# Gate scores of the tokens on VectorE instead of TensorE, in a cross-attention and mixture-of-experts kernel on one core

## What is computed

```python
x = x + xattn(layernorm(x), ctx_768, w_q, w_k, w_v, w_o, b_o)   # 64 x 128 tokens of 256; 16 heads of 64
x = x + ffn(layernorm(x), gate, W1, b1, W2, b2)

def xattn(x, context, ...):
    q, k, v = x @ w_q, context @ w_k, context @ w_v
    attn = softmax(q k^T * SCALE)
    return (attn v) @ w_o + b_o

def ffn(x, gate, ...):
    raw_gate = softmax(x @ gate)                 # 8 experts
    keep the two best, divide by their sum
    return sum over the two experts of weight * (relu(x @ W1[e] + b1[e]) @ W2[e] + b2[e])
```

## Time and profile before

| what | value |
|---|---|
| time, median of 3 runs | 1654.01 us (1653.54 to 1655.09) |
| the profiled execution: its time, its span | 1657.4 us, 1655.6 us |
| mean granted TensorE clock | 0.995 |
| busy PE, DVE, ACT, POOL | 1619.5, 1267.8, 1188.3, 808.9 us |
| TensorE in the chain that ended last | 70% of the span |
| the eight gate products, L1459 | 256 products, passes -1 to 30, first at 22.7 us, last at 1150.6 us |

### The profile page before, as it was taken

How to read it: one execution, slowest core, us unless ns; L and a number is a source line. 1 busy time by engine, 2 the same in 40 slices (tenths; PEclk the granted TensorE clock), 3 DMA queues, 4 the chain that set the end, 5 groups by cost and what they waited for, 6 DMA issues and landing times.

```text
span 1655.6 us, 44861 instructions
## 1 busy us (share of the span) xinstructions
PE 1619.5 (98%) x13844; PEld 1540.7 (93%) x13845; DVE 1267.8 (77%) x3309; ACT 1188.3 (72%) x3485; POOL 808.9 (49%) x920
## 2 busy tenths in 40 slices
PE   6999999999999999999999999999799999999997
PEld 6899999999999999999999999999799999999997
DVE  6677888777788877777887777778678777777775
ACT  5777777777777777777777777777566777777674
POOL 4244454454444445444444544444436555555555
PEclk9999999999999999999999999999999999999999
DMA  8032111112211111221111122111489855555554
GB/s 266 16 90 71 57 57 57 57 65 93 71 57 57 57 57 64 87 78 58 57 57 57 64 80 83 61 57 45 148 240 260 180 88 89 82 89 88 84 85 63
DMA packets 106299, 144.01 MB, mean 87 GB/s; under 512 B 12752, under 2 KB 88656, under 8 KB 106128
## 3 DMA queue, kind: packets, MB, share of 16 engines
q1 hardware_dynamic: 60800, 87.95, 16.4%
q0 software_dynamic: 26816, 37.32, 12.8%
q10 hardware_dynamic: 18640, 18.19, 4.1%
HBM read 76.05 MB, written 67.38 MB: 87 GB/s over the span
## 4 chain that ended last, share of the span: by engine, by line
PE 70%; issue 7%; DVE 7%; DMA 5%; DVEq 3%; POOL 2%; ACT 2%; POOLq 1%; ACTq 1%; SPq 0%
PE bank_a L1362 33%; PE bank_s L1362 11%; PE bank_t L1369 8%; PE bank_v L1395 8%; DMA out<-stage_room,number 5%; DVE hid L1290 3%; DVE stage_room L1307 3%; PE bank_a L1427 2%; PE bank_a L1428 2%; PE bank_a L1435 2%; PE bank_a L1436 2%; PE bank_a L1459 2%; DVEq L1302 1%; POOL out L713 1%; DVEq L1281 1%
## 5 line engine op out<-in xcount | busy, mean ns | idle before, releaser
L642 POOL TENSOR_TENSOR prob<-prob,inv 128x512 f32<-128x512 f32 x256 | 271.1, 1059 | 600.6 <-DVE inv L937 597.5
L755 ACT ACTIVATE prob<-bank_s,low 128x128 f32<-128x128 f32 x1024 | 361.7, 367 | 189.5 <-DVE low L932 186.1
L932 DVE TENSOR_REDUCE low<-bank_s 128x4 f32<-128x512 f32 x256 | 176.3, 689 | 208.9 <-PE bank_s L1362 206.4
L713 POOL DMA_INDIRECT out<-stage_room,number x142 | 230.8, 1625 | 53.8 <-issue 53.2
L755 ACT ACTIVATION_READ_ACCUMULATOR prob<-bank_s,low 128x1 f32 x1024 | 210.7, 206 | 0.0
L866 ACT ACTIVATE hidt_h<-hid 128x512 fp32r<-128x512 f32 x142 | 89.7, 632 | 125.7 <-DVE hid L1290 123.8
L959 DVE TENSOR_TENSOR kt_l<-bank_a,kt_h 64x512 fp32r<-64x512 f32 x256 | 173.3, 677 | 3.1 <-ACT kt_h L772 1.2
L1369 PE MATMUL bank_t<-ident,prob 128*128 128x128 f32 x1024 | 161.0, 280 | 9.6 <-POOL prob L642 9.5
L1362 PE MATMUL bank_s<-kt_l,qt_h 128*128 128x256 f32 x512 | 165.3, 323 | 0.0
L748 ACT ACTIVATE probt<-bank_t 128x512 f32<-128x512 f32 x256 | 152.8, 597 | 8.6 <-issue 6.2
L772 ACT ACTIVATE kt_h<-bank_a 64x512 fp32r<-64x512 f32 x256 | 151.5, 592 | 4.9 <-PE bank_a L1362 3.4
(11 more groups left out here) (227 smaller groups left out, 5291.8 us busy)
## 6 DMA issues: line engine op xcount, KB each, us to landing
stage_room<-lists ACTq DMA_DIRECT2D x67, 265.0 KB
halves<-stage_room SPq DMA_DIRECT2D x32, 512.0 KB
homes<-halves SPq DMA_DIRECT2D x16, 1024.0 KB, 5.6
xin<-in_x SPq DMA_DIRECT2D x32, 256.0 KB, 2.7
stage_room<-in_x SPq DMA_DIRECT2D x32, 256.0 KB
stage_room<-in_w SPq DMA_DIRECT2D x32, 256.0 KB, 4.1
out<-stage_room SPq DMA_DIRECT2D x32, 256.0 KB, 2.2
cin<-in_ctx SPq DMA_DIRECT2D x32, 128.0 KB, 2.4
```

The lines of the kernel that those rows point to most:

```text
L642: pool.tensor_tensor(prob[:, n % 4, :, :], prob[:, n % 4, :, :], wide(inv[:, n % 4, :], P), ALU.mult).then_inc(s_norm.sem, 1)
L713: pool.indirect_dma_start(out, bass.IndirectOffsetOnAxis(ap=number[:, u, b:b + 1], axis=0), ysum[:, u, b, :], None, compute_op=ALU.add).th ...
L755: e = act.activation(prob[:, n % 4, h, :], bank_s[n % 2][:, h * P:(h + 1) * P], ACT.Exp, bias=low[:, n % 4, h:h + 1], scale=-1.0, accum_ou ...
L932: dve.tensor_reduce(low[:, n % 4, :], bank_s[n % 2][:, :].rearrange("p (h k) -> p h k", h=4), AX.X, ALU.min).then_inc(s_low.sem, 1)
```

## The change

VectorE makes the tokens' part itself, from passes 1 to 30. For each block b and expert e it multiplies the raw tokens `xin[:, b, :]` (128 x 256) with `gate_b[:, e, :]`, the centred gate column laid out over all 128 partitions, and the sum over the 256 goes to `x_two[:, b, e]` by `accum_out`; the products themselves go to `junk`. These are sixteen operations a pass, five at the end of slot 1, six of slot 2, three of slot 3 and two of slot 5. In slot 7 a copy takes the place of the reduction and the two scalings. TensorE's eight products stay in passes -1 and 0 alone. `gate_b` is a 1 MB load into `wo_t`'s room, issued by SyncE in pass 0 ahead of fourteen other loads and stores, and centred by one 128x2048 operation in slot 6 of pass 0. From pass 2 on `load_x` waits for the last of the sixteen too, which is in slot 5.

```diff
+            gate_b = wo_t.rearrange("p n c -> p (n c)").rearrange("p (e d) -> p e d", e=E)
...
+            def by_products(it):
+                return isinstance(it, int) and it < 1
...
+            junk = in_stage(0, 11, D)
...
                         wait(sp, c_lo, it - 1, "c")
                         wait(sp, ln1_step, it - 1, "ln1")
+                        if not isinstance(it, int) or it > 1:
+                            sp.wait_ge(x_twice, it + 1)
                         load_x(it)
...
                 body(0)
+                sp.wait_ge(wo_t_in, 16)
+                wait(sp, a_full, 0, "o1")
+                sp.dma_start(gate_b.rearrange("p e d -> p (e d)"), gate_t.rearrange("e d -> (e d)")
+                             .rearrange("(o n) -> o n", o=1).to_broadcast([P, E * D])).then_inc(gate_b_in, 16)
                 for k in range(SPARES):
...
-                        if has(it, NEXT):
+                        if has(it, NEXT) and not by_products(it):
+                            dve.wait_ge(x_twice, it + 2)
+                            wait(dve, pool_step, it, "x_gate")
+                            last = dve.tensor_copy(x_gate[:, :, :], x_two[:, :, :])
+                        elif has(it, NEXT):
...
+                def x_scores(it, first, many):
+                    if first == 0 and isinstance(it, int) and it == 1:
+                        dve.wait_ge(gate_b_made, 1)
+                    if first == 11:
+                        dve.wait_ge(x_begun, it)
+                    for k in range(first, first + many):
+                        b, e = k // E, k % E
+                        last = dve.scalar_tensor_tensor(junk[:, k % 11, :], xin[:, b, :], 1.0, gate_b[:, e, :],
+                                                        ALU.mult, ALU.mult, accum_out=x_two[:, b, e:e + 1])
+                    if first == 0:
+                        last.then_inc(x_begun, 1)
+                    if first + many == 2 * E:
+                        last.then_inc(x_twice, 1)
+                X_SCORES = {1: (0, 5), 2: (5, 6), 3: (11, 3), 5: (14, 2)}
...
+                        if isinstance(it, int) and (it, n) == (0, 6):
+                            dve.wait_ge(gate_b_in, 16)
+                            dve.wait_ge(gate_made, 4)
+                            dve.tensor_tensor(gate_b, gate_b, wide(gate_less, D), ALU.add).then_inc(gate_b_made, 1)
...
+                        if n in X_SCORES and has(it, NEXT) and not by_products(it):
+                            x_scores(it, *X_SCORES[n])
...
                     else:
-                        if has(it, NEXT):
+                        if has(it, NEXT) and by_products(it):
                             for b in range(2):
                                 part = dst[:, (4 + 2 * b) * E:(6 + 2 * b) * E]
```

More of the change, by code:

```diff
@@ L71, in wait, with program @@
         engine.wait_ge(signal.sem, value - back)
-def program(nc, x, ctx, w_q, w_k, w_v, w_o, w_ot, b_o, b_oc, gate, w12, b1, b2, out):
+def program(nc, x, ctx, w_q, w_k, w_v, w_o, w_ot, b_o, b_oc, gate, gate_t, w12, b1, b2, out):
     tokens, D = x.shape
@@ L197, in program @@
             gate_hl = sb("gate_hl", [P, DC, 2, E], F32R)
-            bo_col, bo_gate = sb("bo_col", [P, DC]), sb("bo_gate", [P, E])
+            bo_col, gate_rows = sb("bo_col", [P, DC]), sb("gate_rows", [P, 2 * E])
+            gate_less, bo_gate = gate_rows[:, 0:E], gate_rows[:, E:2 * E]
             x_two, x_gate = sb("x_two", [P, 2, E]), sb("x_gate", [P, 2, E])
@@ L310, in program @@
             gate_in, wo_t_in, x_twice = sem("gate_in"), sem("wo_t_in"), sem("x_twice")
+            gate_b_in, gate_b_made, x_begun = sem("gate_b_in"), sem("gate_b_made"), sem("x_begun")
             WEIGHTS = [([w_q[c * P:(c + 1) * P, :]], wq[0][:, c, :], wq[1][:, c, :]) for c in range(DC)]
@@ L1131, in body @@
                             dve.wait_ge(gate_mean, 2)
-                            dve.tensor_copy(bo_gate[:, :], bank_v[:, E:2 * E]).then_inc(gate_made, 1)
+                            dve.tensor_copy(gate_rows[:, :], bank_v[:, 0:2 * E]).then_inc(gate_made, 1)
+                        if isinstance(it, int) and (it, n) == (0, 6):
+                            dve.wait_ge(gate_b_in, 16)
+                            dve.wait_ge(gate_made, 4)
+                            dve.tensor_tensor(gate_b, gate_b, wide(gate_less, D), ALU.add).then_inc(gate_b_made, 1)
                         if isinstance(it, int) and (it, n) == (0, 6):
@@ L1622 @@
         "b_oc": np.ascontiguousarray(np.ascontiguousarray(L0_xattn_b_o).reshape(2, P).T),
-        "gate": L0_ffn_gate,
+        "gate": L0_ffn_gate, "gate_t": np.ascontiguousarray(np.ascontiguousarray(L0_ffn_gate).T),
         "w12": np.concatenate([
```

## The result

| | before | with the change |
|---|---|---|
| median | 1654.01 us (13 runs) | 1643.18 us (13 runs, 1641.05 to 1651.62) |
| ratio to before | | 0.9939, 95% interval 0.9929 to 0.9949 |
| the profiled execution: time, span | 1657.4, 1655.6 us | 1643.29, 1641.5 us |
| busy PE, DVE | 1619.5, 1267.8 us | 1597.0, 1433.6 us |

The change makes the kernel faster by 10.8 us, or 0.6%. The time lies just inside the range, at its lower end, but the forecast was slower, and that is wrong. The time is that of the first rival, within 2 us.

The account below looks back on a forecast made before the run. TensorE was taken as the bound at 36.32 us a pass; with products at 0.41 us VectorE would become it at 36.50, 0.18 more, 5.4 us in 30 passes: 1654.0 + 5.4 = 1659.4 us, range 1643 to 1698.

Parts of the forecast that it names:

- the first rival: VectorE's read of the sum is hidden: a product costs 0.33 to 0.35 us, 36.02 a pass, 1645 us, faster; chance 0.2.
- TensorE as the bound: First stage: TensorE sets the pace at 36.32 us a pass; the eight products removed are 0.81 us, all on its path.
- The wait for `g_mask`: Slot 7: TensorE's next product waits for VectorE's `g_mask`, so 0.30 us a pass come back, not 0.81; floor 36.02 us.
- The price of a product: VectorE, slots 1, 2, 3 and 5: each of sixteen products costs s = 0.33 + 0.08 = 0.41 us start to start.
- Half rate: Rival: VectorE's products run at half rate by the skill's rule, s = 0.68, 40.49 us a pass, 1779 us; chance 0.06.
- The dearer product: Rival: VectorE's product costs 0.47 to 0.49 us, from the bias operation's 0.40 plus the read; 1685 to 1693 us; chance 0.2.
- The formula: First stage: period = 30.76 + 14s us, s being a product's price, never under 36.02; with s = 0.41 it is 36.50.
- Side effects: VectorE: GpSimd's multiplication delays slot 2's products 0.28 us; slot 7's copy saves 0.12; centring `gate_b` costs nothing, at most 2.2.

Follow-up runs that it names:

- e8: Kernel before without the eight gate products, reduction and scalings from pass 1, `g_mask` ahead of `ot_l` (slot 6), `ot_l` ahead of `vv` (slot 0): 1629.53 us.
- e3: Kernel before without the eight gate products, the reduction and the two scalings from pass 1 on, nothing in their place: 1645.38 us.
- e4: Kernel before without the eight gate products, reduction and scalings from pass 1 on, and `g_mask` ahead of `ot_l` in slot 6: 1636.51 us.
- e10: Changed kernel with only the swap in slot 0, `ot_l` ahead of the copy `vv`: 1645.74 us.
- e6: Changed kernel with the sixteen products writing no sum: 1643.61 us.
- e5: Changed kernel with the constant 1.0 of the sixteen products replaced by a column of ones in SBUF: 1651.18 us.
- e1: Changed kernel with `g_mask` made ahead of the subtraction `ot_l` in slot 6: 1639.51 us.
- e7: Changed kernel with `g_mask` ahead of `ot_l` in slot 6 and `ot_l` ahead of the copy `vv` in slot 0: 1634.22 us.
- e11: e7 with one of the sixteen products moved from slot 1 to slot 5: 1631.58 us.

## Why the prediction was wrong

**TensorE as the bound, 0.81 us on the path.** Right. With nothing else in the way it comes back in full (e8: 36.32 to 35.50).

**The wait for `g_mask`.** Right, in place and size: it was forecast to leave a floor of 36.02 us, and the pass is 35.96; e3 has the same floor with nothing added to VectorE. Of the 0.82 us between 36.32 and 35.50 some 0.35 arrive in the changed kernel, and the rest is lost in slot 7, to `g_mask` alone (5.36 instead of 4.88). Taking that wait away gives back 0.25 only (e3 to e4), since 0.22 then go to the `ot_l` of slot 0 (e4 to e8). The forecast had no term for the last, and needed none, since it hides behind the first (e10).

**The price of a product: the first step that failed.** The forecast was s = 0.33 + 0.08 = 0.41, with the read of the sum taken as time of its own, from ScalarE's 0.09 and from VectorE's load of internal state. It is 0.345. The product itself was sized rightly at 0.33 (0.335 in e6), and the separate read is there; but on VectorE the next product starts beside it, and what it adds is 0.01. With 0.345 the forecast's own formula gives 30.76 + 14 x 0.345 = 35.59, under its floor of 36.02, and so 1645 us: VectorE doesn't become the bound. The first rival had this price and this time. Its heading, a read that is hidden, is what the trace shows; its condition, a sum written within the product, is not, since the read is an instruction of its own, 480 times in the run. No row of the kernel before had VectorE read an accumulator, so its price was taken across engines, from one that doesn't overlap it.

**Half rate.** Wrong, and with it, for this operation, the rule that the prediction quotes for it: two fp32 inputs in SBUF and an accumulator run at 0.345 us for 256 elements, where half rate needs 0.53. **The dearer product:** the row of 0.40 was real, but its cause is the scalar from memory (e5), which this operation doesn't have. (The bias's neighbour L1290, read as 0.41 a piece, is 0.39 from start to start: the row after its four begins at 1406.57, 1.57 us after 1405.00.)

**The formula: the second step that failed.** It was never reached in the changed kernel, but e5 checks it. At 0.405 it gives 36.43, and the pass is 36.16. From slot 4 to slot 6 it had 8.30 and the run 634.46 - 626.15 = 8.31; from slot 6 to slot 1 12.95 and 647.36 - 634.46 = 12.90. The other 0.23 are in slots 1 to 3, forecast at 3.52 + 1.61 + 4.10 + 0.28 + 14 x 0.405 = 15.18 and measured at 626.15 - 611.20 = 14.95. Slot 1 is 0.10 longer than forecast (5.65), and two terms were too large. Slot 2 takes 621.05 - 616.85 = 4.20 us instead of 4.32: its first product, which meets GpSimd's multiplication, takes 618.96 - 618.46 = 0.50 instead of 0.405, 0.10 more where the forecast has 0.28 (in the changed kernel 0.51 instead of 0.345, 0.17 more). And slot 3 takes 5.10 instead of 5.32, since its work of 4.10 had a wait in it that carries no bracket: the operation behind `qt_l` reads what TensorE has just made, and in the kernel before it started 0.81 us after `qt_l`, 0.04 us after the end of TensorE's last product (625.56 + 0.28 = 625.84). In e5 it starts 0.61 us after `qt_l`. The kernel before, VectorE and TensorE, then e5:

```profile
625.07 0.69 DVE L951 SCALAR_TENSOR_TENSOR qt_l<-bank_a,qt_h 128x512 fp32r<-128x512 f32 x1
625.88 0.43 DVE L972 TENSOR_TENSOR stage_room<-bank_a,stage_room 128x264 f32<-128x264 f32 x1
```

```profile
625.56 0.28 PE L1362 MATMUL bank_a<-wo_h,ot_h 128*128 128x264 f32 x1
```

```profile
623.13 0.69 DVE L972 SCALAR_TENSOR_TENSOR qt_l<-bank_a,qt_h 128x512 fp32r<-128x512 f32 x1
623.74 0.42 DVE L993 TENSOR_TENSOR stage_room<-bank_a,stage_room 128x264 f32<-128x264 f32 x1
```

So the forecast of slower would have failed even at its own price: at 0.405 the change comes out about even (e5: 0.13% under the kernel before), not 0.3% slower. The formula was steep (420 us for each us of s), and its sign turned at 0.40, next to the value taken: 36.50 is only 0.18 over 36.32, less than the 0.27 by which e5 shows the rest of the sum to be too long. A forecast with this margin was too sure of its sign.

**Side effects.** The copy in slot 7 saves little, as forecast: VectorE's work in that slot falls from 5.31 to 5.13 us, 0.18 instead of 0.12. The copy lasts 1.02 us, to 603.05, and GpSimd's subtraction runs to 601.74 + 1.28 = 603.02; that the one waits for the other is read from these ends, no run tests it. The centring of `gate_b` in pass 0 takes 2.28 us, and nothing of it shows in the time, since the 30 passes explain the gain.

```profile
601.74 1.28 POOL L692 TENSOR_TENSOR stage_room<-stage_room 128x512 fp32r<-128x512 f32 x1
```

**What is left between the pairs.** The 0.07 us a pass between e1 and e4 lie in slot 1 (5.51 and 5.44), in the wait for `ot_l`. They are not the sixteen products' cost, which come later in the pass: from slot 7's `low` to slot 0's `ot_l` VectorE takes 6.45 us in e1, with the copy of `x_gate` in it, and 6.38 in e4, which has no such copy. The 0.18 between e7 and e8 lie in slot 2, and go with the place of one product in slot 1 (e11). What stays open are the 0.10 us of e5's slot 1, and 2 of the 8 us by which e5 is slower than the changed kernel.

## What to carry to other kernels

When an engine at its limit is relieved, look at the next instruction in its queue that waits for a result of another engine, and at when that result is made: here over half of what was taken off came back as a wait for a result that had been early enough before. Two swaps in the other engine's order and one product moved released all of it. Such waits stand one behind the other, so that removing the second alone shows nothing. And where a forecast's sign hangs on the price of one instruction that the trace doesn't show, a price taken over from another engine is a bound, not a value. Where the sign turns next to the value taken, the errors of all the other terms have to be smaller than that distance too.

## What the runs showed of the hardware

- A read of VectorE's accumulator lasts 0.08 us and runs beside the start of the next product: a product of 128x256 with its sum costs 0.345 us from start to start (changed kernel), without it 0.335 (e6). On ScalarE the read costs 0.09 of its own.
- A scalar from memory instead of a constant adds 0.06 us to this operation of VectorE (0.345 to 0.405, e5).
- How to read the view: a short wait for another engine may carry no bracket. In slot 3 of the kernel before 0.12 us between the end of one operation and the start of the next had none, while 0.16 us in front of slot 1's `low` had one; the difference was seen only when the operation came earlier in another kernel.
